# Values of the first attention projected inside its steps; the second attention keeps all four split contexts in SBUF

## What is computed

```
# layer 0: 16 heads of 64, LoRA on q, k, v, o, and 4 image tokens at the end of the context
q_in = x @ Wq + lora(x)
k_in = org_ctx @ Wk + lora(org_ctx);  v_in = org_ctx @ Wv + lora(org_ctx)      # 508 tokens
out = attention(q_in, k_in, v_in) + attention(q_in, ipa_ctx @ Wk_ipa, ipa_ctx @ Wv_ipa)
x = x + (out @ Wo + bo + lora(out))
x = x + mixture_of_experts(layernorm(x))          # 8 experts, top 2
# layer 1: 8 heads of 64, all 512 tokens
x = x + attention(layernorm(x) @ Wq, ctx @ Wk, ctx @ Wv) @ Wout + bout
x = x + bit_ffn(layernorm(x))
```

## Time and profile before

| | us |
|---|---|
| median of 3 runs | 1253.2 (1248.27 to 1254.41) |
| the profiled execution, its own time | 1245.08 |
| its span | 1243.3 |
| mean granted clock of TensorE | 0.898 |
| PE busy | 950.8 (76%) |
| ACT busy | 757.0 (61%) |
| DVE busy | 724.9 (58%) |
| POOL busy | 649.8 (52%) |

### The profile page before, as it was taken

One profiled execution on the slowest core, in us unless ns is written; L12 is line 12 of the kernel. 1 busy time (PEld: TensorE's weight loads), 2 busy tenths in 40 slices (PEclk: granted clock), 3 DMA queues, 4 the chain that ended last, 5 costly groups with the idle time before them and its releaser, 6 DMA issues. The chain is left out here.

```text
span 1243.3 us, 24205 instructions
## 1 busy us (share of the span) xinstructions
PE 950.8 (76%) x9167; PEld 734.3 (59%) x9174; DVE 724.9 (58%) x1302; ACT 757.0 (61%) x1265; POOL 649.8 (52%) x563
## 2 busy tenths in 40 slices
PE   3976789899989989985515999907778888961675
PEld 3755567676767667764414999905456666751344
DVE  2553557657655766654274444456466665638776
ACT  2453868868876887881433444304678787834576
POOL 1330856767675667670376555303467676733122
PEclk9988999999999999996656999958899999975889
DMA  9740999999998999992342222144499899962001
GB/s 261 275 170 6 184 185 178 178 210 159 178 184 172 158 182 155 156 169 52 119 143 85 73 82 73 56 144 173 79 181 166 158 156 158 165 103 101 5 26 39
DMA packets 444193, 171.01 MB, mean 138 GB/s; under 512 B 410128, under 2 KB 427728, under 8 KB 444048
## 3 DMA queue, kind: packets, MB, share of 16 engines
q1 hardware_dynamic: 440336, 159.23, 64.1%
q0 software_dynamic: 3744, 10.23, 2.6%
HBM read 49.68 MB, written 19.05 MB: 55 GB/s over the span
## 5 line engine op out<-in xcount | busy, mean ns | idle before, releaser
L467 POOL TENSOR_TENSOR A_PHL<-A_pr,A_PHL 128x508 f16<-128x508 f32 x256 | 295.3, 1158 | 171.3 <-ACT A_pr L772 171.0
L977 DVE TENSOR_REDUCE A_negmax<-A_ps 128x2 f32<-128x1016 f32 x128 | 155.4, 1214 | 75.7 <-PE A_ps L605 75.2
L467 POOL TENSOR_TENSOR C_PHL<-C_pr,C_PHL 128x512 f16<-128x512 f32 x128 | 148.3, 1165 | 89.4 <-ACT C_pr L772 89.0
L771 ACT ACTIVATE A_PHL<-A_ps,A_negmax 128x508 f16<-128x508 f32 x256 | 179.6, 701 | 20.2 <-DVE A_negmax L977 19.2
L772 ACT ACTIVATE A_pr<-A_ps,A_negmax 128x508 f32<-128x508 f32 x256 | 181.3, 708 | 0.0
L623 PE MATMUL A_ps<-A_VH,A_PT 128*128 128x65 bf16 (+1 forms) x1024 | 109.6, 197 | 38.1 <-DMA A_PT<-A_PHL 37.9
L623 PEld LDWEIGHTS A_ps<-A_VH,A_PT 128*128 128x128 f16 (+1 forms) x1024 | 93.7, 98 | 66.7 <-DMA A_PT<-A_PHL 54.3
L605 PE MATMUL A_ps<-A_K,A_Q 64*128 64x508 f32 x768 | 124.5, 429 | 11.1 <-ACT A_pr L772 9.0
L624 PE MATMUL A_ps<-A_VL,A_PT 128*128 128x64 f16 (+1 forms) x1024 | 108.8, 194 | 0.0
L625 PE MATMUL A_ps<-A_VH,A_PT 128*128 128x65 bf16 (+1 forms) x1024 | 108.6, 195 | 0.0
L977 DVE TENSOR_REDUCE C_negmax<-C_ps 128x2 f32<-128x1024 f32 x64 | 78.2, 1222 | 43.0 <-PE C_ps L605 42.8
(11 more groups left out here) (353 smaller groups left out, 2740.2 us busy)
## 6 DMA issues: line engine op xcount, KB each, us to landing
A_PT<-A_PHL SPq DMA_TRANSPOSE x256, 3.4
M_rin<-in_L_ffn_w_in SPq DMA_DIRECT2D x8, 512.0 KB, 3.7
M_rout<-in_L_ffn_w_out SPq DMA_DIRECT2D x8, 512.0 KB, 4.0
...
```

The costliest lines, as they stand in the source:

```text
L467: pool.tensor_tensor(PHL[:, e % PRING, 1, 0:KEYS], pr[:, e % RING, 0:KEYS], PHL[:, e % PRING, 0, 0:KEYS], ALU.subtract).then_inc(pl_ready. ...
L771: a.activation(PHL[:, e % PRING, 0, 0:KEYS], o, ACT.Exp, bias=nm[:, n % 4, h:h + 1])
L977: v.tensor_reduce(nm[:, g % 4, :], ps[:, S_BANK + 2 * (g % 2):S_BANK + 2 * (g % 2) + 2, 0:KEYS], AX.X, ALU.max, negate=True).then_inc(max_ ...
```

## The change

- A: a batch's values are projected by half batches (a half is heads 0 to 7 or 8 to 15) inside the steps, each into the part of the single buffer `VH[0]`, `VL[0]` whose old values are used up. The prologue keeps four `v` jobs, the first half of batch 0; 28 move to steps 3, 4, 15, 17 (second half of this batch) and 20, 31, 32, 33 (first half of the next). `store_v` and `load_v` are gone.
- A: there are two `CT` tiles. Contexts 0 and 1 stay in them; 2 and 3 are split in `O` (`spare`), stored, and loaded in step 29 of batches 0 and 1. The prologue's order on all engines is written anew.
- A: the image tokens' context (`ci`) is laid out on the host so that one DMA of contiguous rows loads it; `VWO` is loaded per batch; `SI` and `mi` lie in `xn`.
- C: four `CT` tiles, all loaded at the start, ahead of the weights q and o; no context load in the steps. The first four jobs after the values use the four value banks.

```diff
             plan(s0 + 4 * c - 2, "k", b, c)
         if ipa:
+            for kt, u in enumerate((3, 4, 15, 17)):
+                plan(s0 + u, "v", b, 2 * kt + 1)
+            if b + 1 < B:
+                for kt, u in enumerate((20, 31, 32, 33)):
+                    plan(s0 + u, "v", b + 1, 2 * kt)
...
+    v_jobs = [("v", 0, 2 * kt) for kt in range(QT)] if ipa else [("v", b, kt) for b in range(B) for kt in range(QT)]
     first = [("x", 0, 0), ("x", 0, 1), ("q", 0, 0), ("k", 0, 0)]
     jobs = v_jobs + first + [u for s in sorted(at) for u in at[s]]
     JOB = {u: n for n, u in enumerate(jobs)}
     HI = {u: n for n, u in enumerate([u for u in jobs if u[0] not in "siy"])}
-    NV = len(v_jobs)
+    NV = len(v_jobs) + len(first)
...
-        CT = sb("CT", [P, 3, N], FR)
+        CT = [sb(f"CT{k}", [P, 3, N], FR) for k in range(2 if ipa else B)]
...
-        VBUFS = 2 if ipa else B
-        VH = [sb(f"VH{k}", [P, QT, heads, DH + 1], BF16) for k in range(VBUFS - 1 if ipa else VBUFS)]
-        VL = [sb(f"VL{k}", [P, QT, heads, DH], F16) for k in range(VBUFS - 1 if ipa else VBUFS)]
-        first_use = ExitStack()
-        with first_use:
-            WV = [sb(f"WV{s}", [P, 2, HD], FR, first_use) for s in "hl"]
-        if ipa:
-            VH.append(sb("VH1", [P, QT, heads, DH + 1], BF16))
-            VL.append(sb("VL1", [P, QT, heads, DH], F16))
+        VH = [sb(f"VH{k}", [P, QT, heads, DH + 1], BF16) for k in range(1 if ipa else B)]
+        VL = [sb(f"VL{k}", [P, QT, heads, DH], F16) for k in range(1 if ipa else B)]
+        WV = [sb(f"WV{s}", [P, 2, HD], FR) for s in "hl"]
...
+            CTV = [CT[0][:, :, :], CT[1][:, :, :], spare, spare]
+            SI = xflat[:, 0:(QT + 1) * HIPA].rearrange("p (g t) -> p g t", t=IPA)
+            mi = xflat[:, (QT + 1) * HIPA:(QT + 1) * HIPA + QT * heads]
+            ci = pr[0:CR, 2, 0:2 * B * IPA].rearrange("p (c n) -> p c n", c=2)
...
+            def load_craw(b):
+                if b >= 2:
+                    wait(sp, ct_split, 4 if b == 2 else 6)
+                sp.dma_start(craw[b], ctx_t[:, :, b * N:(b + 1) * N]).then_inc(craw_loaded[min(b, 2)].sem, 16)
+
+            def store_ct(b):
+                wait(sp, ct_split, 2 * (b + 1))
+                sp.dma_start(scratch["ct"][b], CTV[b].bitcast(F32)).then_inc(ct_stored[b].sem, 16)
+
+            def load_ct(b):
+                sp.dma_start(CT[b % len(CT)][:, :, :].bitcast(F32), scratch["ct"][b]).then_inc(ct_loaded[b].sem, 16)
+
...
                 weight("v")
                 load_craw(0)
+                sp.dma_start(ci, w["ipa_ctx"]).then_inc(ipa_loaded.sem, 16)
                 sp.dma_start(WI, w["k_ipa"]).then_inc(ipa_loaded.sem, 16)
                 sp.dma_start(WJ, w["v_ipa"]).then_inc(ipa_loaded.sem, 16)
-                for kc in range(2):
-                    sp.dma_start(ci[:, kc, :].rearrange("p (b t) -> p b t", t=IPA), w["ipa_ctx"][:, kc, :, :]).then_inc(ipa_loaded.sem, 16)
...
                 store_ct(0)
+                store_ct(1)
                 load_craw(2)
-                for kt in range(QT):
-                    store_v(0, kt)
-                store_ct(1)
                 wait(sp, vwo_filled, 1)
                 weight("k")
+                store_ct(2)
                 load_craw(3)
-                for kt in range(QT):
-                    store_v(1, kt)
-                store_ct(2)
-                store_ct(3)
-                for kt in range(QT):
-                    store_v(2, kt)
                 wait(sp, vwo_copied, 1)
                 sp.dma_start(scratch["vwo"], VWOT.rearrange("p (c n) -> p c n", n=D)).then_inc(vwo_stored.sem, 16)
+                store_ct(3)
                 wait(sp, vwo_stored, 16)
-                for c in range(OC):
-                    sp.dma_start(VWO[c * 2 * IPA:(c + 1) * 2 * IPA, :, :],
-                                 scratch["vwo"][:, c, :].rearrange("(b x) n -> x b n", b=B)).then_inc(vwo_loaded.sem, 16)
+                load_vwo(0)
             else:
-                for name in "vk":
-                    weight(name)
-                for j in range(2):
-                    sp.dma_start(CTV[(j + 1) % 2].bitcast(F32), scratch["ct"][VORDER[j]]).then_inc(ct_loaded[(j + 1) % 2].sem, 16)
-                for name in "qo":
-                    weight(name)
+                weight("v")
+                weight("k")
+                for b in range(B):
+                    load_ct(b)
+                weight("q")
+                weight("o")
                 sp.dma_start(bias[:, :], w["bias"]).then_inc(bias_loaded.sem, 16)
-                for j in range(2, B):
-                    wait(sp, pj_filled, JOB["v", VORDER[j - 2], QT * HALVES - 1] + 1)
-                    sp.dma_start(CTV[(j + 1) % 2].bitcast(F32), scratch["ct"][VORDER[j]]).then_inc(ct_loaded[(j + 1) % 2].sem, 16)
...
-                if b + 1 < B:
-                    if ipa and 6 <= u < 6 + QT:
-                        load_v(b + 1, u - 6)
-                    if u == U - 7:
-                        if ipa and b == 0:
-                            wait(sp, ct_stored[0], 32)
-                        wait(sp, pj_filled, JOB["k", b, PAIRS - 1] + 1)
-                        sp.dma_start(CT[:, :, :].bitcast(F32), scratch["ct"][b + 1]).then_inc(ct_loaded[0].sem, 16)
+                if ipa and u == 29 and b + 2 < B:
+                    wait(sp, pj_filled, JOB["k", b, PAIRS - 1] + 1)
+                    wait(sp, ct_stored[b], 16)
+                    load_ct(b + 2)
+                if ipa and u == 18 and b:
+                    wait(sp, pj_filled, JOB["y", b - 1, 2 * QT - 1] + 1)
+                    load_vwo(b)
...
+                if ipa and b >= 2 and k == 0:
+                    wait(pe, ct_loaded[b], 16)
+                t = CT[b % len(CT)]
+                five(bank(("v", b, k)), lambda o, x, kc, s, a, z: mm(
+                    o, t[:, x, kt * P:(kt + 1) * P], WV[s][:, kc, half * BANK:(half + 1) * BANK],
+                    start=a, stop=z)).then_inc(pj_filled.sem, 1)
...
+                if ipa and n % 16 == 0:
+                    wait(pe, pj_free, JOB["v", b, 2 * (QT - 1) + n // 16 % 2] + 1)
+                vh, vl = VH[b % len(VH)], VL[b % len(VH)]
...
                 wait(pe, w_split, 1)
-                values(0)
+                wait(pe, ct_split, 2)
+                for u in v_jobs:
+                    project_v(u[1], u[2])
                 image_values()
-                values(1, 0, 4)
                 wait(pe, vwo_copied, 1)
                 lora("q")
-                values(1, 4, 8)
                 lora("k")
-                values(2)
+                turn_x(0, 0)
+                turn_x(0, 1)
                 turn_weight()
-                values(3, 0, 4)
                 image_weight()
-                values(3, 4, 8)
+                wait(pe, w_split, 4)
             else:
                 wait(pe, w_split, 1)
-                for j in range(B):
-                    values(j)
-            for kc in range(KC):
-                turn_x(0, kc)
-            wait(pe, w_split, 4 if ipa else 3)
+                for u in v_jobs:
+                    if u[2] == 0:
+                        wait(pe, ct_loaded[u[1]], 16)
+                    project_v(u[1], u[2])
+                turn_x(0, 0)
+                turn_x(0, 1)
+                wait(pe, w_split, 3)
             project_q(0, 0)
...
+                    if ipa and b:
+                        wait(a, pv_done, (b - 1) * U + 16 * half + 16)
                     m = BANK // DH
-                    vh = VH[0 if ipa else b]
-                    copy(vh[:, kt, half * m:(half + 1) * m, 0:DH], filled(u).rearrange("p (h d) -> p h d", d=DH)).then_inc(pj_hi.sem, 1)
+                    copy(VH[b % len(VH)][:, kt, half * m:(half + 1) * m, 0:DH],
+                         filled(u).rearrange("p (h d) -> p h d", d=DH)).then_inc(pj_hi.sem, 1)
...
+                if ipa and n == 0:
+                    wait(a, ct_split, 2 * B)
...
                 ct_high(1)
                 w_high("o")
-                values(0)
+                for u in v_jobs:
+                    high(u)
                 ct_high(2)
                 wait(a, vwo_filled, 1)
                 copy(VWOT, ps[0:B * 2 * IPA, 0:4, :].rearrange("p a n -> p (a n)")).then_inc(vwo_copied.sem, 1)
-                values(1, 0, 4)
+                ln_act()
                 w_high("q")
-                values(1, 4, 8)
-                ct_high(3)
-                ln_act()
                 w_high("k")
-                values(2)
+                high(first[0])
+                high(first[1])
                 wait(a, wqt_filled, 1)
                 for k in range(2):
                     last = copy(WQT[k].rearrange("p c n -> p (c n)"), ps[:, 2 * k:2 * k + 2, :].rearrange("p a n -> p (a n)"))
                 last.then_inc(wqt_copied.sem, 1)
-                values(3, 0, 4)
                 wait(a, ws_filled, 1)
```

(21 more changed lines are left out.)

150 lines of the change are left out of this document (50 added, 100 removed).

## The result

The changed kernel takes 1215.5 us in the median of 4 runs (1208.93 to 1217.82), beside 1252.7 for the kernel before (1248.27 to 1254.41): a ratio of 0.971, with an interval of 0.967 to 0.975. The forecast was 1211, so the time is 4 us above it and well inside the range.

A forecast was written before the change was run, and what follows sets the result against it. The prediction saw A's prologue as one chain over all engines, and PE as busiest but not full in the steps. Terms -35 (A's prologue), +5 (A's steps), +1 (C's prologue), -13 (C's steps) gave 1253.2 - 42 = 1211 us, range 1193 to 1232.

The forecast's parts named there:

- A's prologue, chain: First attention's prologue: with 28 of 32 value jobs gone, first scores at 83.6 instead of 116.9 us, taking off 33.
- cold prologue: Rival, chance 0.06: in A's prologue PE runs turned weight, image weight and first projections at low clock; 7 us more, 1218.
- The image tokens' context: A's prologue: one load of 128-byte runs replaces two of 16-byte runs; 2 us of PE's 10.48 us wait saved (0 to 4).
- A's steps: First attention's steps: 28 value jobs added, 24 value loads and one context load removed; +5 us (-7 to +25).
- I take 0.7 us a job: +20: A's steps: each of 28 added value jobs costs 0.7 us of its 1.17 us PE time; bounds 11 and 33.
- Relief 15 (8 to 18): A's steps: time saved by dropping value and context loads, 7 us in batch 0, the rest in batches 1 and 2.
- C's prologue: Second attention's prologue: context loads ahead of weights q and o cost 2, free value banks give back 1; +1 (-1 to +5).
- C's steps: Second attention's steps: three context loads go, 4.3 us each with waits and slow matmuls; -13 us (-8 to -15).
- What would show it: The prediction's list of signs in the new profile: times and waits expected in both attentions if it holds.
- hidden: Rival, chance 0.16: PE's idle 34.8 us take most jobs, relief is 18; A's steps -7 or less, 1199 and below.
- slower than before: Rival, chance 0.02: PE at low clock in light steps, 2.55 us a job, total 1269; decides from 2.2 us a job.

The follow-up runs named there:

- run with a busy PE: The changed kernel with 53 matmuls into a bank nobody reads, in PE's waits of the first attention's prologue: 1205.8 us, ratio 0.966.
- one-product kernel: The changed kernel with one matmul instead of five in each of the 28 value jobs in the first attention's steps: 1213.4 us, ratio 0.968.
- kernel with C's values first: The changed kernel, where in C's prologue ACT copies four values ahead of the q weight's high part and two more ahead of o's: 1208.0 us, ratio 0.969.

## Why the forecast was right, and where its steps were not

- **A's prologue, chain (-33 forecast, -29 measured).** The mechanism was right: 28 value jobs leave the chain, and the order of links came as written. No kernel put the jobs back into the prologue; this is read from the rows. Two terms were mis-sized. The turned weight was taken at 5.5 us; PE took 7. The image weight was taken at 4.4 us, its time in the kernel before at a mean clock of 0.87; here the clock was at 0.50 ahead of it, and it took 7.0. The run with a busy PE shows that this is the clock: 3.7 and 3.8 us. The links up to the q weight's low part came 1.2 us shorter than forecast. That leaves the first scores 2.5 us late, 47.6 us behind the merge of o instead of 45.2. Most of the rest comes from the profile of before that the forecast was read from: this stage took 79.4 us in it, and 77.1 and 78.7 in the two others. The "cold prologue" was made a rival of its own with 0.06, where it is a part of the likeliest case.
- **The image tokens' context (-2 forecast).** In eleven profiles the merge of the o weight lies 0.6 us earlier on average, among executions that differ by 6. That is not told from nothing. The context is no longer what PE waits for; the weight behind it is.
- **A's steps (+5 forecast, +5.6 measured).** That the sum came out is luck. "I take 0.7 us a job: +20" failed, and so did its lower bound of 11: four of a job's five matmuls cost 2.7 us over all 28 jobs. What is left of a job, with its copies on ACT and DVE, I estimate from the kernel before without value loads, 434.6 us, against the one-product kernel's 439.7: 5 us, so some 8 in all. "Relief 15 (8 to 18)" is not borne out by the profiles, which give 1 to 6, and not ruled out by the medians, which give 7 to 15. The forecast price was read from PE's idle time in each stretch, and I missed that a fuller PE gets a higher clock for everything else it does. I also read the transposes as nearly all of that idle time; they were 32.2 of 43.9 us, and PE waited 9.0 for ACT. The relief was read from one stretch of batch 0, where it was about right (7 forecast, 5 to 6 measured), and then carried to stretches that show none in the profiles.
- **C's prologue (+1 forecast, +1.3 measured).** The first value's copy starts 17.1 us behind C's first load, 15.0 before: the two microseconds that were put on the queue. The prediction saw that ACT copies no value before the o weight's high part, and took that order as given; it was the larger term, as the kernel with C's values first shows.
- **C's steps (-13 forecast, -10.5 measured).** Shown by taking the loads out (half of the change alone) and by putting them back: 3.5 us a load and not 4.3.
- **What would show it.** First scores at 80 to 86 us: 88.07 in the first profile, which is a miss, and 82 to 87 in the others (73.8 with the busy PE). Light stretch of 25.5 to 27: 26.5. Waits for transposes below 34.8: 17.1 in all of A. Batch 0's steps 8 to 15 at 27: 28.3. C's first value copy at 853 to 858 was meant on the time axis of before: 17.1 us behind C's first load is 855.6 there. No wait over 3 us in C's steps: the longest for transposes is 2.6 (3.5 before); one wait of 3.5 us for ACT in C's third step stands in both kernels.

By the stages the forecast is 8.4 us too good: A's prologue 5, C's steps 2.5, the rest 1. By the medians it is only 4.7 (37.3 us for 42). The 3.7 us between the two are not placed, so part of the closeness of 1215 to 1211 is luck. Of the rivals, "hidden" was right on the price of the jobs (most cost next to nothing); whether its relief of 18 was wrong by 3 us or by more than 10 stays open. In the rival "slower than before" the other terms add up to -47, so 2.0 us a job would have met them, not 2.2.
